# One kernel of six layers: linear attention's reciprocals made by VectorE ahead of phi's maximum, and background quantised layers in operations of two tiles with the bias added in four

## The reference, cut to what matters

```python
x = x + 0.5 * L0_ffn(layernorm(x))     # quantised linear layer, "QA"
x = x + L0_attn(layernorm(x))          # linear attention
x = x + 0.5 * L0_ffn(layernorm(x))     # quantised linear layer, "QB"
x = x + 0.5 * L1_ffn(layernorm(x))     # routed MLP, "FA"
x = x + L1_attn(layernorm(x))          # softmax attention, 16 heads
x = x + 0.5 * L1_ffn(layernorm(x))     # routed MLP, "FB"
# L0_ffn:  x_scale = max(max|x| over a row / 127, 1e-12); x_q = round(x / x_scale)
#          y = (x_q @ w_q.T) * x_scale * w_scale + bias
# L0_attn: q, k, v = x @ W.T + b; sq, sk = elu(q) + 1, elu(k) + 1     ("phi", 16 query and 4 key heads of 128)
#          norm = sq . sum(sk); attn = sq @ (sk.T @ v) / (norm + 1e-6); out = attn @ Wo.T
```

## Time and profile before

| | |
|---|---|
| median of three runs | 3464.34 us |
| the profiled execution | 3464.4 us |
| its span | 3462.6 us |
| TensorE busy in it | 3349.7 us (97%) |
| VectorE busy | 2670.0 us (77%) |
| ScalarE busy | 2047.5 us (59%) |
| GpSimd busy | 1056.2 us (31%) |

### The profile page before, as it was taken

The page is one execution under the profiler, slowest core; times in us unless marked ns, Lnnn a source line. Parts: engine busy times, 40 slices in busy tenths (PEclk is TensorE's granted clock), DMA queues, the critical chain, the costliest instruction groups (busy, mean ns, idle before and its releaser), DMA issues.

```text
span 3462.6 us, 52979 instructions
## 1 busy us (share of the span) xinstructions
PE 3349.7 (97%) x19526; PEld 2859.8 (83%) x19526; DVE 2670.0 (77%) x4949; ACT 2047.5 (59%) x3904; POOL 1056.2 (31%) x1274
## 2 busy tenths in 40 slices
PE   6899999999999999999999999999999999999997
PEld 4788788778888888888888888888888888888885
DVE  6898896767876778876778677886788867876776
ACT  4677777655556565556555656555555565556553
POOL 4786667622122122122121222212212131212112
PEclk9999999999999999999999999999999999999999
DMA  2222112110000000000000101000000010001000
GB/s 86 79 77 62 56 61 75 55 31 16 13 25 25 13 13 15 13 25 25 13 13 13 28 27 32 13 16 24 26 14 14 14 33 28 16 16 31 28 17 23
DMA packets 98526, 104.22 MB, mean 30 GB/s; under 512 B 10336, under 2 KB 88800, under 8 KB 98144
## 3 DMA queue, kind: packets, MB, share of 16 engines
q1 hardware_dynamic: 98272, 100.85, 9.7%
HBM read 87.18 MB, written 13.63 MB: 29 GB/s over the span
## 4 chain that ended last, share of the span: by engine, by line
PE 71%; DVE 5%; ACT 3%; issue 0%; POOL 0%; DVEq 0%; ACTq 0%; POOLq 0%
PE at_ps_job L2019 12%; PE at_ps_job L35 7%; PE at_ps_job L37 7%; PE at_ps_job L36 7%; PE at_ps_o L35 6%; PE at_ps_o L37 6%; PE at_ps_o L36 6%; PE at_ps_s L35 6%; PE at_ps_s L36 6%; PE at_ps_s L37 6%; DVE at_neg_max L1946 1%; ACT x_resident L1770 1%; DVE at_probT_lo L1813 1%; PE at_ps_job L653 1%; DVE li_wkv_lo L1844 0%; ACT at_probT_hi L1729 0%
## 5 line engine op out<-in xcount | busy, mean ns | idle before, releaser
L1729 ACT ACTIVATE at_probT_hi<-at_ps_job 128x512 fp32r<-128x512 f32 x1024 | 611.3, 598 | 890.1 <-PE at_ps_job L2019 887.6
L1813 DVE TENSOR_TENSOR at_probT_lo<-at_ps_job,at_probT_hi 128x512 fp32r<-128x512 f32 x1024 | 702.6, 686 | 275.3 <-ACT at_probT_hi L1729 264.7
L1770 ACT ACTIVATE x_resident<-at_ps_s,at_neg_max 128x1024 f32<-128x1024 f32 x512 | 570.7, 1115 | 151.3 <-DVE at_neg_max L1946 146.1
L1704 POOL TENSOR_TENSOR li_wkv_hi<-li_bkv,ch_cols 128x256 fp32r<-128x256 f32 x252 | 154.3, 612 | 1631.5 <-PE at_ps_job L37 1580.8
L1946 DVE TENSOR_REDUCE at_neg_max<-at_ps_s 128x1 f32<-128x1024 f32 x512 | 622.0, 1215 | 5.2
L2019 PE MATMUL at_ps_job<-ident,x_resident 128*128 128x128 f32 x4096 | 613.8, 272 | 4.9 <-DVE at_probT_lo L1813 3.3
L2019 PEld LDWEIGHTS at_ps_job<-ident,x_resident 128*128 128x128 f32 x4096 | 495.9, 140 | 97.7 <-issue 7.1
L35 PE MATMUL at_ps_o<-at_probT_hi,at_v_lo 128*128 128x512 f32 x1024 | 446.3, 436 | 8.9 <-DVE li_wkv_lo L1844 7.7
L35 PE MATMUL at_ps_s<-at_k_hi,at_q_lo 128*128 128x512 f32 x1024 | 445.1, 435 | 0.0
L37 PE MATMUL at_ps_o<-at_probT_lo,at_v_hi 128*128 128x512 f32 x1024 | 404.7, 395 | 0.0
L36 PE MATMUL at_ps_s<-at_k_hi,at_q_hi 128*128 128x512 f32 x1024 | 402.0, 393 | 0.0
(11 more groups left out here) (356 smaller groups left out, 7461.1 us busy)
## 6 DMA issues: line engine op xcount, KB each, us to landing
li_bkv<-attn_w SPq DMA_DIRECT2D x256, 128.0 KB, 2.3
li_bkv<-mlp_w SPq DMA_DIRECT2D x112, 128.0 KB, 2.3
li_wo_hi<-li_wo_kept SPq DMA_DIRECT2D x24, 256.0 KB, 2.6
li_wo_lo<-li_wo_kept SPq DMA_DIRECT2D x24, 256.0 KB, 3.0
li_wq_hi<-li_wq_kept SPq DMA_DIRECT2D x48, 128.0 KB, 2.2
li_wq_lo<-li_wq_kept SPq DMA_DIRECT2D x48, 128.0 KB, 2.3
x_resident<-x SPq DMA_DIRECT2D x4, 1024.0 KB, 13.4
out<-x_resident SPq DMA_DIRECT2D x4, 1024.0 KB, 4.9
```

The source lines that it names most:

```text
L1704: nc.gpsimd.tensor_tensor(hi, src, none, ALU.add).then_inc(s_wh[part], 1)
L1729: nc.scalar.activation(ph[:, i // TC, 4 * half:4 * half + 4, (i % TC) * P:(i % TC + 1) * P], c.turned_bank(2 * TB * u + 2 * i + half), ACT ...
L1770: nc.scalar.activation(prob[:, slot % 2, :], ps_s[slot % 2][:], ACT.Exp, bias=nmax[:, slot:slot + 1], accum_out=rsum[:, u % 2, slot:slot + ...
L1813: nc.vector.tensor_tensor(pl[at], c.turned_bank(2 * TB * u + 2 * i + half), ph[at].bitcast(F32), ALU.subtract).then_inc(s_pl, 1)
```

## The change: what it does

First part, linear attention: ScalarE's copy of the norm columns is gone. VectorE reads them from the OUT banks itself (one or two instructions of `ALU.add` with 1e-6) and makes the reciprocal, both between the background slice and phi's maximum; for that it waits for OUT of the step (`s_y`). `li_rnorm` has two buffers. The x additions stay behind phi's maximum.

Second part, quantised layers in the background: layernorm of two tiles in each of s = 4 to 7; magnitudes of two tiles in each of 5 to 8; scales and reciprocals of four tiles in 6 and in 8; the bias added to two tiles in each of 5 to 8; ScalarE's scaling two tiles in each of 7 to 10.

```diff
@@ pool_background
-        if s == 6:
-            pool.wait_ge(c.q_xn, TB * (n + 1))
-            at = c.group(b, 0, TB)
-            nc.gpsimd.tensor_tensor(at, at, sh.bias_half[:].unsqueeze(1).to_broadcast([P, TB, D]), ALU.add).then_inc(c.q_bias, 1)
+        if 5 <= s < 9:
+            j = s - 5
+            pool.wait_ge(c.q_xn, TB * n + 2 * j + 2)
+            at = c.group(b, 2 * j, 2 * j + 2)
+            nc.gpsimd.tensor_tensor(at, at, sh.bias_half[:].unsqueeze(1).to_broadcast([P, 2, D]), ALU.add).then_inc(c.q_bias, 1)
@@ act_background
-        if s in (8, 10):
-            if s == 8:
-                act.wait_ge(c.q_rec, n + 1)
-            for j in range(s // 2 * 4 - 16, s // 2 * 4 - 12):
+        if 7 <= s < 11:
+            if s in (7, 9):
+                act.wait_ge(c.q_rec, 2 * n + s // 2 - 2)
+            for j in (2 * s - 14, 2 * s - 13):
@@ dve_background
-        if s in (4, 5):
-            for j in range(4 * s - 16, 4 * s - 12):
+        if 5 <= s < 9:
+            lo = 2 * (s - 5)
+            dve.wait_ge(c.q_xn, TB * n + lo + 2)
+            nc.vector.tensor_reduce(c.amax[:, lo:lo + 2], c.tiles[:, lo:lo + 2, :], AX.X, ALU.max,
+                                    apply_absolute_value=True).then_inc(c.q_amax, 1)
+        if 4 <= s < 8:
+            for j in (2 * s - 8, 2 * s - 7):
                 layernorm_tile(nc, sh, c.tiles[:, j, :], c.x(b, j), j).then_inc(c.q_xn, 1)
-        if s in (6, 7):
-            lo = 4 * (s - 6)
-            dve.wait_ge(c.q_xn, TB * n + lo + 4)
-            nc.vector.tensor_reduce(c.amax[:, lo:lo + 4], c.tiles[:, lo:lo + 4, :], AX.X, ALU.max,
-                                    apply_absolute_value=True).then_inc(c.q_amax, 1)
-        if s == 7:
+        if s in (6, 8):
...
@@ linear_attention_phase, scalar
-                if y_step(t):
-                    act.wait_ge(s_y, t - LAG + 1)
-                    if t > LAG:
-                        act.wait_ge(s_rn, t - LAG)
-                    for own, banks in out_banks(t - LAG):
-                        last = nc.scalar.activation(norm[:, own], ps[:, banks, D], ACT.Copy, bias=ATT_EPS)
-                    last.then_inc(s_norm, 1)
@@ linear_attention_phase, vector
                 dve_background(nc, dve, sh, c, t)
+                if y_step(t):
+                    m = t - LAG
+                    dve.wait_ge(s_y, m + 1)
+                    for own, banks in out_banks(m):
+                        nc.vector.tensor_scalar(norm[:, own], ps[:, banks, D], ATT_EPS, None, ALU.add).then_inc(s_norm, own.stop - own.start)
+                    dve.wait_ge(s_norm, TC * (m + 1))
+                    if m >= 2:
+                        dve.wait_ge(s_y3, m - 1)
+                        dve.wait_ge(s_x, 3 * m - 3)
+                    nc.vector.reciprocal(rnorm[:, m % 2, :], norm[:]).then_inc(s_rn, 1)
                 if q_step(t):
                     dve.wait_ge(s_eq, t + 1)
                     nc.vector.scalar_tensor_tensor(f[:, t % 2, :], c.own_bank(("QUERY", t)), bias[:, 1, t // 2 % H:t // 2 % H + 1], f[:, t % 2, :],
                                                    ALU.add, ALU.max).then_inc(s_f, 1)
                 if y_step(t):
                     m = t - LAG
-                    dve.wait_ge(s_norm, m + 1)
-                    if m:
-                        dve.wait_ge(s_y3, m)
-                        dve.wait_ge(s_x, 3 * m)
-                    nc.vector.reciprocal(rnorm[:], norm[:]).then_inc(s_rn, 1)
```

More of the change, by code:

```diff
@@ L382, in pool_background @@
     if kind in QUANT:
-        if s == 6:
-            pool.wait_ge(c.q_xn, TB * (n + 1))
-            at = c.group(b, 0, TB)
-            nc.gpsimd.tensor_tensor(at, at, sh.bias_half[:].unsqueeze(1).to_broadcast([P, TB, D]), ALU.add).then_inc(c.q_bias, 1)
+        if 5 <= s < 9:
[3 more added lines that the diff above has]
+            nc.gpsimd.tensor_tensor(at, at, sh.bias_half[:].unsqueeze(1).to_broadcast([P, 2, D]), ALU.add).then_inc(c.q_bias, 1)
         if 14 <= s < 18:
             j = s - 14
-            pool.wait_ge(c.q_bias, n + 1)
+            pool.wait_ge(c.q_bias, 4 * n + j + 1)
             pool.wait_ge(c.taken, c.plan.by_dve["QP", n, j])
@@ L565, in dve_background @@
     if kind in QUANT:
-        if s in (4, 5):
-            for j in range(4 * s - 16, 4 * s - 12):
-                layernorm_tile(nc, sh, c.tiles[:, j, :], c.x(b, j), j).then_inc(c.q_xn, 1)
-        if s in (6, 7):
-            lo = 4 * (s - 6)
-            dve.wait_ge(c.q_xn, TB * n + lo + 4)
-            nc.vector.tensor_reduce(c.amax[:, lo:lo + 4], c.tiles[:, lo:lo + 4, :], AX.X, ALU.max,
-                                    apply_absolute_value=True).then_inc(c.q_amax, 1)
-        if s == 7:
[L575 to L578, removed]
+        if 5 <= s < 9:
[5 more added lines that the diff above has]
+            for j in (2 * s - 8, 2 * s - 7):
+                layernorm_tile(nc, sh, c.tiles[:, j, :], c.x(b, j), j).then_inc(c.q_xn, 1)
+        if s in (6, 8):
+            h = s // 2 - 3
+            at = slice(4 * h, 4 * h + 4)
+            dve.wait_ge(c.q_amax, 4 * n + 2 * h + 2)
+            nc.vector.tensor_scalar(c.scale[:, at], c.amax[:, at], 1.0 / QMAX, 1e-12, ALU.mult, ALU.max).then_inc(c.q_sc, 1)
+            dve.wait_ge(c.q_sc, 2 * n + h + 1)
+            nc.vector.reciprocal(c.rec[:, at], c.scale[:, at]).then_inc(c.q_rec, 1)
     if kind in ROUTED:
@@ L994, in linear_attention_phase @@
         norm = sb("norm", [P, TC], F32)
-        rnorm = sb("rnorm", [P, TC], F32)
+        rnorm = sb("rnorm", [P, 2, TC], F32)
         ybuf = sb("ybuf", [P, 2, D], F32)
@@ L1262, in _ @@
                         act.wait_ge(s_x3, m - 1)
-                    nc.scalar.activation(ybuf[:, m % 2, :], c.own_bank(("OUT", m, 3))[:, 0:D], ACT.Copy, scale=rnorm[:, 3:4]).then_inc(s_y3, 1)
+                    nc.scalar.activation(ybuf[:, m % 2, :], c.own_bank(("OUT", m, 3))[:, 0:D], ACT.Copy,
+                                         scale=rnorm[:, m % 2, 3:4]).then_inc(s_y3, 1)
                 if made_time.get(t + 1, 2 * KVH) < 2 * KVH:
@@ L1354, in _ @@
                         x = x_tile_of(m, j)
-                        nc.vector.scalar_tensor_tensor(x, c.own_bank(("OUT", m, j))[:, 0:D], rnorm[:, j:j + 1], x, ALU.mult, ALU.add).then_inc(s_x, 1)
+                        nc.vector.scalar_tensor_tensor(x, c.own_bank(("OUT", m, j))[:, 0:D], rnorm[:, m % 2, j:j + 1], x, ALU.mult, ALU.add).then_inc(s_x, 1)
         @block.tensor
```

## The result

Four runs of the changed kernel gave 3443.17 to 3444.94 us, median 3443.62; the kernel before gave 3464.84 on the same chip. The ratio is 0.9936 (95% interval 0.9924 to 0.9948). The forecast was 3451.9, so 8.3 us of gain were not foreseen. The profiled execution took 3444.0 us, its span is 3442.3.

The account below looks back on a forecast made before the run. TensorE, busy 97% of the span, was taken as the bound, with losses where it waits for VectorE or its clock falls. Terms -17.6 + 3.6 + 1.5 - 1.0 + 3.0 - 2.0 = -12.5 took 3464.4 to 3451.9 us, range 3441 to 3462.

Parts of the forecast that it names:

- bias in four, its pieces and the backlog: Linear phase: shorter keys' maxima and restored clock -17.6 us, quarters holding VectorE +3.6, late GpSimd work +1.5.
- tiles spread: Slices 4 and 5 lose normalised tiles, 6 and 7 gain them: -1 us, between -3 and +2.
- norm on VectorE: 0.15 us more VectorE a step, costing where VectorE never idles: 1.9 us between 396 and 447 us, 1.1 elsewhere, +3.0.
- early reciprocal, ScalarE's chain: Near the linear phase's end, `li_phi_hi` starts sooner after phi's maximum: -0.45 us on some five steps, -2.
- Where VectorE idles ahead of phi's maximum: VectorE waits for ScalarE's exp, 49 times, 50.8 us; early norm and reciprocal fit there if OUT is done: -2 us.
- the chain through ScalarE is worth more: Rival, 10%: 31 waits for phi's maximum each fall a further 0.25 us, 8 us go: 3444 us.
- The sign that was to show it: Between 396 and 447 us, a stretch some 2 us longer was to show the norm's cost.
- The hold: GpSimd's whole bias addition held three keys' maxima about 5 us; 13.2 us of TensorE idling and 6.4 of clock at stake.
- near 22 us with none above 2: Sign for the linear phase: TensorE's waits for phi's maximum in total, and their longest, if the forecast was right.
- The hold is paid in pieces: Rival, 15%: the same hold of VectorE reappears in quarters; a third of that gain remains, 3459.7 us.
- Phi's maximum behind OUT: Rival, 8%: VectorE waits for OUT before phi's maximum, TensorE for phi's maximum; 22 us on top, 3474 us.
- The backlog: GpSimd overfull in steps 6 to 9, `li_phi_lo` late: +1.5 us, shown by waits for it around steps 9 to 11.

Follow-up runs that it names:

- e3: Kernel before with only the bias addition cut in four, in slices 5 to 8; VectorE's four tiles a slice as before: 3463.54 us, ratio 0.9995.
- e2: Kernel before with the background part of the change alone (tiles, magnitudes, scales and bias spread over slices 4 to 8): 3453.62 us, ratio 0.9968.
- e1: Kernel before with the linear attention part alone (norm and reciprocal on VectorE ahead of phi's maximum), bias in one addition: 3454.89 us, ratio 0.9969.
- e5: Kernel before with only the reciprocal moved ahead of phi's maximum; ScalarE still copies the norm, background as before: 3450.05 us, ratio 0.9949.
- e7: Kernel before with only ScalarE's list changed, `li_ybuf` behind `li_phi_hi` of the next step: 3453.74 us, ratio 0.9962.
- e4: Kernel before with the linear attention part alone, but `li_ybuf` on ScalarE also waits for phi's maximum of its step: 3475.58 us, ratio 1.0031.
- e12: Changed kernel with the norm left on ScalarE, reciprocal still early, bias additions in slices 5 to 8: 3435.03 us, ratio 0.9914.
- e9: Changed kernel with bias additions in slices 10 to 13 and the norm left on ScalarE, reciprocal still early: 3431.43 us, ratio 0.9903.

## Why the prediction was right, and where it was not

The sign held, and the time lies in the range. The size was off by 8.3 us, because one term was mis-sized by far, the norm's cost was too low, and two others were wrong and cancelled; that last is luck.

| term | predicted | medians | ratios x 3465 us |
|---|---|---|---|
| bias in four, its pieces and the backlog | -12.5 | -2.5 | -1.7 (e3, alone) |
| tiles spread | -1.0 | -9.9 | -9.4 (e2 against e3) |
| norm on VectorE | +3.0 | +4.8 | +6.9 (e1 against e5) |
| early reciprocal, ScalarE's chain | -2.0 | -17.6 | -17.7 (e5) |
| sum | -12.5 | -25.2 | -21.9 |
| the change itself | | -21.2 | -22.2 |

The medians of two sets do not add up to the change; the ratios do, to 0.3 us, which is closer than their intervals warrant.

*The step that failed* is "Where VectorE idles ahead of phi's maximum". It read the right mechanism from rows 11, `li_phi_hi` 1.25 us behind phi's maximum because `li_ybuf` stands before it, and counted -0.45 a step. But it applied this to "some five steps where TensorE also waits" near the phase's end. The runs show it over the whole phase: ScalarE's order alone is worth 13.9 us (e7), 3.1 of them in steps 61 to 72, far from the phase's end. What the step left out is GpSimd. It looked for a wait of VectorE or TensorE, but a late `li_phi_hi` also sets when GpSimd's `li_phi_lo` and x addition run, and so which of VectorE's operations they hold: VectorE's busy time fell by 12.6 us in e7 with not an instruction less. VectorE's waits for `li_m_hi`, which I suspected after the result, are not it (12.7 us against 14.3). The rival "the chain through ScalarE is worth more" named the early `li_ybuf` and gave 3444, with only 10%; that this is the measured time is partly luck, for it put 8 us on the shorter waits for phi's maximum and on ScalarE's missing instruction. TensorE's waits for phi's maximum fell by 5.0 us in the change, and e5 has its gain with that instruction in place.

*The norm on VectorE* was costed soundly in the busy stretch, 1.9 us between 396 and 447 us foretold, 2.2 between steps 61 and 72 measured as the difference of e1 and e5 (56.58 and 54.41), and too low elsewhere: 1.1 us foretold, 2.6 by medians and 4.7 by ratios. The sign that was to show it failed all the same: the stretch became shorter, since the other term was acting there too.

*The hold.* No keys' maximum is above 2 us, as foretold. That TensorE would then no longer wait was wrong: 30.8 us in 30 waits against "near 22 us with none above 2", and a clock of 0.61 where 0.9 was foretold. The held operation was one part of an overfull step; with it gone, the tiles that moved into slices 6 and 7, the quarters beside them and a scale (L579) of 1.14 us filled the same steps. At the three places the idle times went from 16.4 us (the 13.2 and 3.17 just ahead of the first) to 4.04 + 1.30 + 2.84 + 2.27 + 1.94 = 12.4. In e2, steps 0 to 13 are 1.6 us shorter than before, steps 31 to 37 (slices 8 to 14 of QA of batch 3) 4.3 and steps 49 to 54, the third place, 3.8. The 4.3 the prediction had not counted at all, and which part of the spread gives them is not shown. *Bias in four* is not as empty as its -2.5 looks: in e3 the linear phase, the only one that this term spoke of, gained 8.1 us, and the softmax phase gave 7.7 back where four tiles stood in one slice. *Tiles spread*, put at -1 as a guess with bounds of -3 and +2, got most of its -9.9 by keeping this loss away, in a phase that the prediction had set aside.

*Rivals.* "The hold is paid in pieces" was true in the case that the prediction did not look at, four tiles in a slice (e3: 0.98 us a slice). "Phi's maximum behind OUT" did not come: VectorE waited 46.8 us for OUT with the norm, but 5.5 instead of 50.8 for exp, and steps 92 to 100 took as long as before to 0.03 us. The backlog did not show: no wait for `li_phi_lo` of TensorE near steps 9 to 11. The softmax phase had the same length within 1.3 us.

*Left open.* Why e4, with the norm early and only `li_ybuf` late, is 10 us slower than the kernel before. How e5's and e1's gains divide between VectorE's shorter operations and its shorter waits: in e5, VectorE is busy 20.2 us less than before between phi's maxima of steps 0 and 127, of which the stretch keeps 15.6. And what GpSimd's quarters cost in slices 5 to 8: 3.6 us by medians with ScalarE's norm (e12 against e9), 1.9 with VectorE's, 3.8 in both cases by ratios, none of it clear of noise.

## What to carry to other kernels

An instruction that only waits can cost more than one that works. Ask of each in-order list what stands behind the waiting instruction, and follow it through every engine: here it made GpSimd late, and GpSimd then held VectorE. Such a cost is in no list of waits. It shows when the same instructions are busy for longer in one trace than in another (27.6 against 23.5 us for 40 tiles), so compare lengths by group before you settle on a wait as the cause. Make a small result ahead of the long operation that does not need it, but leave it on the engine that has time. If a long GpSimd operation holds VectorE, cutting it helps only where the pieces fall beside work that they do not hold: split and spread were worth 2.5 and nothing alone, and 12.5 together.
